# Two attention and feed-forward layers on one core: later integers transposed by DMA, fewer column operations, another order

## What is computed

```
x = x + attention0(layernorm(x), ctx)      # q = ctx Wq + bq, k = ctx Wk + bk, softmax(q k), applied to the rows of x
x = x + ffn0(layernorm(x))                 # 8 bit activations, ternary weights, 1024 hidden, value * silu(gate)
x = x + attention1(layernorm(x), ctx)      # 16 heads of 128, 8 key/value heads, scale 1/sqrt(128), mask
x = x + ffn1(layernorm(x))                 # fp8-rounded weights, 768 hidden, silu(gate) * up, scales
```

## Time and profile before

| | us |
|---|---|
| median of 3 runs | 341.05 (340.27 to 341.25) |
| the profiled execution | 340.63 |
| its span, first to last instruction | 338.8 |
| PE busy | 319.1 (94%) |
| DVE busy | 249.9 (74%) |
| ACT busy | 240.0 (71%) |
| POOL busy | 205.3 (61%) |

### The profile page before, as it was taken

The page is one execution under the profiler, slowest core; times in us unless marked ns, Lnnn a source line. Parts: engine busy times, 40 slices in busy tenths (PEclk is TensorE's granted clock), DMA queues, the critical chain, the costliest instruction groups (busy, mean ns, idle before and its releaser), DMA issues.

```text
span 338.8 us, 6783 instructions
## 1 busy us (share of the span) xinstructions
PE 319.1 (94%) x2257; PEld 283.4 (84%) x2268; DVE 249.9 (74%) x777; ACT 240.0 (71%) x550; POOL 205.3 (61%) x312
## 2 busy tenths in 40 slices
PE   5877899999999999999999999999999999999994
PEld 4565567899999998999998889998999989879784
DVE  3898897898988668878667688866564757776384
ACT  3769987777597898869658956955585889782260
POOL 2767463557689987369887743699634265766000
PEclk9999999999999999999999999999999999999999
DMA  6997002008000000000000000000000000000001
GB/s 181 368 369 247 0 0 64 4 0 297 0 3 1 2 2 0 0 3 1 3 2 0 2 1 3 0 2 0 2 1 2 1 2 0 3 0 3 31 33 62
DMA packets 9490, 14.34 MB, mean 42 GB/s; under 512 B 1136, under 2 KB 6896, under 8 KB 9456
## 3 DMA queue, kind: packets, MB, share of 16 engines
q1 hardware_dynamic: 9456, 13.90, 12.1%
HBM read 12.85 MB, written 1.05 MB: 41 GB/s over the span
## 4 chain that ended last, share of the span: by engine, by line
PE 73%; ACT 9%; POOL 8%; DVE 4%; issue 3%; DMA 2%; SPq 1%; ACTq 0%; DVEq 0%; POOLq 0%
PE pb L1792 44%; PE pb L2009 7%; PE pb L2061 6%; POOL sm L485 4%; PE pb L2104 3%; PE pb L1867 2%; DMA xb<-in_ctxT 2%; ACT sm L771 2%; PE pb L1897 2%; PE pb L1950 1%; PE pb L1959 1%; POOL step L491 1%; PE pb L1852 1%; PE pb L1941 1%; PE pb L1888 1%
## 5 line engine op out<-in xcount | busy, mean ns | idle before, releaser
L485 POOL TENSOR_SCALAR sm<-sm,srec,mask_all 128x256 f32<-128x256 f32 x128 | 71.6, 575 | 59.1 <-DVE srec L1342 59.1
L771 ACT ACTIVATE sm<-sm,smin 128x256 f32<-128x256 f32 x128 | 63.6, 502 | 4.6 <-DVE smin L1336 4.4
L1336 DVE CUSTOM_DVE_ANT_0 sm<-pb,mask_all 128x256 f32<-128x256 f32 x128 | 48.2, 417 | 6.5 <-PE pb L1792 6.5
L1346 DVE TENSOR_TENSOR pT_lo<-pb,pT_hi 128x512 fp32r<-128x512 f32 x64 | 43.2, 683 | 12.6 <-ACT pT_hi L778 12.2
L778 ACT ACTIVATE pT_hi<-pb 128x512 fp32r<-128x512 f32 x64 | 36.8, 593 | 9.9 <-PE pb L2009 9.8
L1792 PE MATMUL pb<-ctx_hi,q_hi 128*128 128x256 f32 x128 | 39.1, 305 | 0.1
L1792 PE MATMUL pb<-n_hi,oT_hi 128*128 128x256 f32 x128 | 38.0, 297 | 0.0
L1792 PE MATMUL pb<-xT_hi,m_hi 128*128 128x256 f32 x128 | 37.8, 295 | 0.2 <-DVE xT_lo L1315 0.2
L2009 PE MATMUL pb<-identf,sm 128*128 128x128 f32 x256 | 35.7, 274 | 1.9 <-POOL sm L485 1.9
L766 ACT ACTIVATE q_hi<-pb 128x512 fp32r<-128x512 f32 x32 | 19.0, 593 | 25.3 <-PE pb L1792 25.1
L1792 PE MATMUL pb<-xT_hi,m_lo 128*128 128x256 f32 x128 | 36.1, 282 | 0.0
(11 more groups left out here) (187 smaller groups left out, 944.7 us busy)
## 6 DMA issues: line engine op xcount, KB each, us to landing
w_raw<-in_w SPq DMA_DIRECT2D x4, 576.0 KB, 5.8
wraw<-in_wgvT SPq DMA_DIRECT2D x4, 512.0 KB, 8.0
xa<-in_x SPq DMA_DIRECT2D x4, 256.0 KB, 3.9
wraw<-in_woutT SPq DMA_DIRECT2D x2, 512.0 KB, 9.9
out<-xb SPq DMA_DIRECT2D x4, 256.0 KB, 2.1
xb<-in_ctxT SPq DMA_DIRECT2D x2, 256.0 KB, 4.4
stage<-in_wk SPq DMA_DIRECT2D x1, 512.0 KB, 9.6
stage<-in_wv SPq DMA_DIRECT2D x1, 512.0 KB, 10.4
```

The source lines that it names most:

```text
L485: g.tensor_scalar(sm[:, n % 2, k, :], sm[:, n % 2, k, :], srec[:, n % 2, k:k + 1], mask_all[:, b, S:S + 1], ALU.mult, ALU.mult).then_inc(n ...
L771: a.activation(sm[:, n % 2, k, :], sm[:, n % 2, k, :], ACT.Exp, bias=smin[:, n % 2, k:k + 1], scale=-1.0, accum_out=ssum[:, n % 2, k:k + 1 ...
L1336: v.tensor_tensor_reduce(out=sm[:, n % 2, k, :], in0=bank(1 + k // 2)[:, (k % 2) * S:(k % 2 + 1) * S], in1=mask_all[:, b, 0:S], scale=1.0, ...
L1346: v.tensor_tensor(pT_lo[:, c, :], bank(3 + c), as_f32(pT_hi[:, c, :]), ALU.subtract).then_inc(pT_lo_done, 1)
```

## The change

1. Integers of later rows and tiles are transposed by DMA. For batches 1 to 3, POOL takes the rounding constant off in a new step `hidden_in(b)` and writes bf16 over rows of xa that are no longer needed; SP's `turn_rows(b)` transposes them into hqT. For tiles 2 to 7, SP's `turn_hidden(j)` transposes uq into uqT. PE's `integers(1..3)` and `hidden(2..7)` and ACT's copies after them are gone; `gate_half`, `value_half` and `ffn_out` wait for the DMA instead.
2. The first rows of x and the two biases are issued by ACT's queue, first thing; SP's list has another order, and `scales` comes after the last `turn_hidden`.
3. The `nmean` columns are gone (POOL subtracts the mean itself); single-column operations of DVE on the two tiles of a batch are merged into one.
4. The sum of the third output piece is done on POOL (`output(2)`).
5. All engines' lists and `PASSING` are in another order.

```diff
+            act.dma_start(xa[:, tiles(0), :], x_v[:, tiles(0), :]).then_inc(ld_x[0], 16)
+            for n, v in enumerate((bq, bk)):
+                act.dma_start(bqk[:, n:n + 1], v.rearrange("(p a) -> p a", a=1)).then_inc(ld_bias, 16)
...
+            def turn_rows(b):
+                sp.wait_ge(hq_done, b)
+                if b >= 3:
+                    sp.wait_ge(value_ps, 2 * TB * (b - 2))
+                    sp.wait_ge(gate_ps, 2 * TB * (b - 2))
+                sp.dma_start(hqT[:, b % 3, :, :].rearrange("p k (t c) -> p (k t) c", c=P), integer_rows(b), transpose=True).then_inc(hq_turned[b], 16)
+
+            def turn_hidden(j):
+                sp.wait_ge(uq_done, j + 1)
+                sp.wait_ge(ffn_ps, j - 1)
+                sp.dma_start(uqT[:, j % 2, :, :], uq[:, j % 2, :], transpose=True).then_inc(uq_turned[j % 2], 16)
...
+            def hidden_in(b):
+                pool.wait_ge(hr_done, b + 1)
+                pool.wait_ge(base_done, TB * (b + 1))
+                g.tensor_scalar(integer_rows(b).rearrange("p (k t c) -> p k t c", k=KD, t=TB),
+                                gbuf[:, b % 2, :, :].rearrange("p t (k c) -> p k t c", k=KD), -ROUND, 1.0, ALU.add, ALU.mult).then_inc(hq_done, 1)
...
             def ffn_out(j):
-                pe.wait_ge(uqT_done, j + 1)
+                if j < TB:
+                    pe.wait_ge(uqT_done, j + 1)
+                else:
+                    pe.wait_ge(uq_turned[j % 2], 16 * (j // 2))
...
-                for t in range(sl.start, sl.stop):
-                    v.tensor_scalar(nmean[:, t:t + 1], mv[:, t, 0:1], -1.0, None, ALU.mult)
...
+            def output(k):
+                pool.wait_ge(dsc_done, k + 1)
+                rows = xb[:, 2 * k:2 * k + 2, :]
+                g.tensor_tensor(rows, y[:, k % 2, :].rearrange("p (t d) -> p t d", d=D), rows, ALU.add).then_inc(y_added, 1)
```

More of the change, by code:

```diff
@@ L389, in _ @@
             eighth(1)
+            turn_hidden(2)
             eighth(2)
+            turn_rows(2)
+            turn_hidden(3)
             eighth(3)
+            turn_rows(3)
+            turn_hidden(4)
+            turn_hidden(5)
+            turn_hidden(6)
+            turn_hidden(7)
             scales()
             for n in range(NT // 2):
-                sp.wait_ge(y_done, n + 1)
+                if n == 2:
+                    sp.wait_ge(y_added, 1)
+                else:
+                    sp.wait_ge(y_done, n + 1 if n < 2 else n)
                 sp.dma_start(out_v[:, 2 * n:2 * n + 2, :], xb[:, 2 * n:2 * n + 2, :]).then_inc(stored, 16)
@@ L542, in _ @@
             normalise(3, 1)
-            outputs_split(2)
+            eighths(0)
+            hidden_in(2)
+            integers(2)
             eighths_out(0)
-            integers(2)
-            outputs_split(3)
             normalise(4, 0)
@@ L648, in _ @@
             rows4(3)
+            output(2)
         @block.scalar
@@ L839, in _ @@
             probs1(2)
-            turned(2)
+            ternary(1)
+            ternary(2)
+            turned(0)
+            turned(1)
             ternary(3)
@@ L1164, in stats @@
                 dve.wait_ge(mv_done, bn_count[0])
[L1165 to L1166 removed]
             def variances(sl, done):
[L1169 to L1171 removed]
+                v.tensor_scalar(ve[:, 0, sl], mv[:, sl, 1], EPS, None, ALU.add).then_inc(done, 1)
             def stats1(b):
@@ L2113, in _ @@
             project1(1)
+            rows1(0)
+            rows1(1)
             energy(0)
+            project1(2)
             energy(1)
-            project1(2)
-            rows1(0)
+            turn_context(1)
             energy(2)
             probs(0)
-            turn_context(1)
+            weight_sum(0)
+            rows1(2)
             mix(0)
-            weight_sum(0)
+            project1(3)
             turn_kv(0)
-            rows1(1)
+            probs(1)
             turn_kv(1)
-            probs(1)
-            project1(3)
+            energy(3)
             turn_kv(2)
-            rows1(2)
             turn_kv(3)
@@ L2175, in _ @@
             rows3(0)
+            turn_queries(7)
             fuse_vo(5)
-            value_half(2, 1)
             queries(0)
             fuse_qk(5)
-            value_half(3, 0)
+            value_half(2, 1)
             scores(0, 0)
@@ L2212, in _ @@
             probs4(2, 1)
+            queries(5)
             scores(4, 0)
@@ L2263, in _ @@
             attn_out(5, 1)
+            gate_half(5, 0)
+            queries(10)
             probs4(7, 0)
             probs4(7, 1)
-            gate_half(5, 0)
-            queries(10)
-            value_half(4, 1)
             scores(9, 0)
@@ L2371, in _ @@
             probs4(17, 1)
+            attn_out(15, 1)
+            queries(20)
             scores(19, 0)
-            queries(20)
+            value_half(7, 1)
             scores(19, 1)
-            attn_out(15, 0)
-            attn_out(15, 1)
             contexts(17, 0)
@@ L2379, in _ @@
             probs4(18, 0)
+            probs4(18, 1)
+            queries(21)
+            scores(20, 0)
             attn_out(16, 0)
-            probs4(18, 1)
-            scores(20, 0)
             scores(20, 1)
             attn_out(16, 1)
-            value_half(7, 1)
-            queries(21)
             attn_out(17, 0)
             contexts(18, 0)
+            attn_out(17, 1)
             contexts(18, 1)
             probs4(19, 0)
-            attn_out(17, 1)
             probs4(19, 1)
             scores(21, 0)
-            hidden(6)
             queries(22)
+            ffn_out(6)
             scores(21, 1)
@@ L2521, in _ @@
             attn_out(31, 1)
+            rows4(2)
             down(0)
```

1213 lines of the change are left out of this document (593 added, 620 removed), and 3 rows, old and new, of the table PASSING.

## The result

The changed kernel is slower: 342.08 us against 340.68 us (medians of 15 runs each, on one chip), a ratio of 1.0036, 95% interval 1.0022 to 1.0049. The forecast was 334.2 us. The executions profiled took 341.42 us (span 339.6) after, near the low end of its 15 runs (341.40 to 342.92), and 340.6 us (span 338.8) before.

The account below looks back on a forecast made before the run. PE was taken as the bound: start of `queries(0)`, fixed PE work, and the end. Terms -3.3 + 1.2 - 4.5 - 0.2 = -6.8 took 340.6 to 333.8 us; the median's 0.4 made 334.2, range 329.5 to 340.5.

Parts of the forecast that it names:

- Transposes off PE: Full stretch, 60 to 310 us: transposes removed from PE save 3.3 us; waits for the DMA give back 1.2.
- the two tiles that I held for tight: Hidden tiles 5 and 7: with 2.8 us of room and 3.5 us to landing, each waits 0.6 us.
- The nine copies: ACT's copies after the removed transposes: eight lie where ACT idles, worth nothing; the ninth is counted in the start.
- `hidden_in`: New POOL step, 128x512, three times: 0.52 us each, at most 1.05; two cost nothing, the first counts within the start.
- SyncE's queue: Loads behind `turn_rows(1)` land by 42 us, some eight us before first use; `scales` also in time: no cost.
- The start: Before `queries(0)`: earlier loads and ternary chain bring it to near 55.4 us, -4.5 us; bounds 6 won, 1 lost.
- The end: Last output pieces: one sum moved from DVE to POOL saves 0.2 us; bounds 0.7 gained, 0.3 lost.
- The reordering: Remaining reordering of the lists: changes only who waits briefly, counted as nothing, bounds 1 us either way.
- A: Rival at `ffn_out`: DMA transposes land late and PE waits, slower from 5.6 us to landing, up to 373 us; chance 0.12.
- B: Rival: the start gives nothing, `queries(0)` stays at 58 to 61 us, total 338.7 us; chance 0.19.

Follow-up runs that it names:

- experiment 1: The changed kernel with the mean negated again and POOL's rows and base adding it instead of subtracting: 332.62 us, and 332.41 us when run again.
- section 9: The comparison of e12 with e11, which differ in the queue issuing the first rows of x and the biases: 334.28 against 333.16 us.
- e11: The kernel of experiment 1 with the first energy product issued ahead of the first two transpositions of context rows: 333.16 us, ratio 0.9767.
- e12: The kernel of e11 with the first rows of x and the two biases issued by SyncE again: 334.28 us, ratio 0.9792.
- experiment 5: The kernel before with only the first rows of x and the two biases issued by ScalarE instead of SyncE: 341.55 us, ratio 1.0020.
- experiment 7: The kernel before, in its own order, with DMA transposes, first rows from ScalarE and merged columns, POOL adding the negated mean: 339.21 us, ratio 0.9949.

## Why the prediction was wrong

The effects, as differences of medians: 340.68 - 1.5 (all parts in the old order) - 6.6 (the order) + 9.5 (the subtraction) = 342.1. The failed step is the third part of the change, which had no term for POOL: measured, it costs 9.5 us. I counted the `nmean` columns as DVE time saved, two of 149 ns a call, and let POOL's side pass as the same instruction with another operand. **The change of operation from `add` to `subtract` had a row neither in the trace nor in my sum**; by my own rule, that what the trace does not show is bounded from both sides, it needed a bound. The trace of before has no subtraction in a two-operation step, but it held a warning that I did not look up. Two steps of the fp8 rounding have one shape; L491 is a maximum and a multiplication, L499 two multiplications (groups by line, kernel before):

```profile
L491 POOL TENSOR_SCALAR step<-step 128x288 f32<-128x288 f32 x16 | 18.8, 1177 | 9.6 <-DVE step L1356 8.7
...
L499 POOL TENSOR_SCALAR step<-sum 128x288 f32<-128x288 f32 x16 | 7.3, 454 | 1.5
```

The first works in place and the second does not, so the pair alone does not prove it, but it says that the operation may set the price on this engine: 1177 against 454 ns. Taken as the upper bound for an operation not yet seen, this ratio of 2.6 would have put 32 x 0.57 x 1.6 = 29 us more on POOL, and the loss on the list of rivals.

Without the subtraction the kernel takes 332.4 to 332.6 us, 1.6 to 1.8 us from the forecast. But this is partly two errors that offset each other, so it does not vindicate the sum:

- *Transposes off PE, -3.3, with waits of 1.2.* The price in the sum was 2.1 us after `queries(0)`. In the old order it is 0.8 there (the last product 1.76 us earlier, `queries(0)` 0.95), with 2.3 us of waits for the DMA; in the new order I see none, so nothing speaks against the whole 3.3, though no run has it apart. From POOL's end to landing it took a hidden tile 2.7 to 3.5 us where I took 3.5; but of the two tiles that I held for tight, 5 and 7, only 7 waits by over 0.35 us, and tile 2 does instead, both in the old order alone. The estimate of 10.5 us by the Trainium skill (VectorE: DVE Perf Modes, The three transpose paths), eight blocks of 1309 ns one after another, falls: eight blocks landed in 2.7 us, of which the issue on SyncE is 1.2. The figure for one block is not refuted, the addition of it is.
- *The nine copies, and `hidden_in`* at 0.62 us against my 0.52: right, nothing seen of either.
- *SyncE's queue.* `raw(8)` landed at 50.35 and not by 42, as `hidden_in(1)` ended at 43.9; its first user ran at 50.66. Nothing lost, by 0.3 us. In experiment 1 it landed at 46.14.
- *The start, -4.5.* This was wrong even without the subtraction: -1.2 and -1.7 us in the two profiles of that kernel. Statistics began 1.2 us sooner (4.76), where I had the rows 2 us sooner. The four gate and value weights were in at 15.62 and 15.94 against 15.71 before; POOL started on the ternary weights at 19.02 and 18.40, not 17.9. The first gate product came at 34.49 and 33.77, not at 32.5. Two readings failed. The weights gained more from ScalarE's issues than I had (2.1 us in section 9: 15.25 in e11, 17.35 in e12), but SyncE's new list set them back by 1.6 (17.35 against 15.71 before). And their landing does not set the ternary chain: in experiment 5 they were in 1.7 us sooner and the chain began 0.5 us later, behind the softmax of the first batches on ScalarE.
- *The end, -0.2.* From the last product to the end of the span it is 5.1 us before and 5.2 in experiment 1: nothing, within my ends.
- *The reordering, 0, bounds 1 us either way.* It was worth 6.6 us, the largest gain of the change. I had named the 2.8 us of idle PE time in the full stretch as all there was to win. Two things were missed: that the transposes in the old order add waits (2.0 us of them in experiment 7) which the new order does not have, and that work moved into the first 60 us shortens the rest, though `queries(0)` starts hardly sooner (58.70, and 58.74 or 58.25). The start of `queries(0)` plus a fixed amount of work was too simple a model.

Of the rivals none was what happened. A, the one on the side that came true, named another mechanism, and that one shows only in the old order, with 2 us; B (the start gives nothing) describes the start almost rightly, and its total of 338.7 is near the 339.2 of experiment 7, which has the old order.

## What to carry to other kernels

Price every operation that changes its code, even when shape, type and count stay the same: on GpSimd a subtract inside a two-operation step took two to three and a half times as long as the add here, and a negated column made once on another engine buys it back. When a change bundles a loss and a gain, undo the one line whose instruction got longer before judging the order around it. And don't explain by a single profile what differs by less than the runs of that kernel differ: two of them showed opposite signs here.

## What the runs showed of the hardware that I had not expected

- GpSimd's `tensor_scalar` with `subtract` in either place: 1.23 us against 0.57 for 128x256 f32, 3.64 against 1.05 for 128x1024. `tensor_tensor` does not have this (808 against 807 ns).
- A DMA transpose within SBUF, 128x1024 bf16, landed 2.7 to 3.5 us after its source was ready, some 1.2 us of which (at most 2.0) are SyncE's issue. Eight 128x128 blocks don't add up. A 128x512 one landed in 2.4 to 3.4 us, but in 4.5 to 6.1 where a load of fp8 weights was still on its way.
- TensorE's granted clock fell to half level from 10.9 to 14.3 us in one execution of a kernel and stayed full there in another of the same kernel.
- The same 512 KB load, `raw(7)`, with no other load on its way, took 3.4 us (experiment 1) to 6.0 us (e11) to land.
- A second issuing queue in the first microseconds delays what is issued first and brings the rest forward: the context 0.6 us later, x 1.2 us sooner, and the last of the same loads 1.9 us sooner (28.12 against 30.06, experiment 5) or 2.6 (28.47 against 31.03, section 9). The median was 0.9 us higher in the one order and 1.1 lower in the other.
